# Attention and routed convolution on Trainium2: the split of x formed earlier on ScalarE and GpSimd, the lower filters' products last in each band

## Chip, cores, metric

The kernel runs on one core of one Trainium2 chip (trn2). The metric is the device time of one execution in microseconds, as the median of several runs; smaller is better.

## What is computed

Sixteen images of 128 channels x 32 x 32, f32, go through two residual blocks. Both begin with a group norm (32 groups of 4 channels, without weights). The first is linear attention, the second a convolution whose 3 x 3 filters are mixed from three experts for each image. Cut to what matters:

```
# block 0: x = x + attention(group_norm(x))
xn  = rmsnorm(xg, g1)                          # over the channels
q, k, v = w_qkv @ xn                           # 4 heads of 32
k, v = concat(memory k, k), concat(memory v, v)   # 4 memory tokens
q = softmax(q, over the 32 of a head) * scale
k = softmax(k, over the tokens)
y = rmsnorm(w_out @ (context(k, v) applied to q) + b_out, g2)
# block 1: x = x + condconv(group_norm(x))
y = relu(rconv(pooled 4 x 4) + bias); gates = sigmoid(relu(fc(y)))   # 3 experts x 128
w = sum over experts of gate_k * expert_weight_k                     # per image
x = x + conv3x3(group_norm(x), w)
```

## The kernel before

**Pipeline.** Every engine has its own queue, written out by hand. `run_steps` calls each engine's `step(t, p)` for t = -1 to 20 (steps 9 to 14 as a loop in pairs); a step holds one call per part, `do(part, t, p, age)`, for image t - age, so that an image passes through several steps and each step works on several images. p is the parity of the buffers. Engines meet through semaphores alone. A queue runs strictly in the order in which `step` names its parts.

**The split of x.** Products of f32 numbers are formed on TensorE from an upper and a lower part: `x_hi` is the value rounded to fp32r, `x_lo` the rest. For the normalised input of block 0, ScalarE forms x_hi (`high1`, L591) from xa, and GpSimd forms x_lo (`low1`, L492) as x minus x_hi. high1 waits until the products of qkv of the image before are done, low1 for x_hi and the same. Both are read by the projections (L1160 to L1162).

**ScalarE's queue** around the change: `filters_first` (first expert by its gate, L662), the last two `qkv_evacuate` (qk from PSUM, L601), `results` of the upper band (PSUM plus the group mean, L684; its tile is called expert_raw in the rows, since it reuses that memory), `filters_high` (w_hi, L668), `q_exponent` (L613), `high1` (L591), `squares1`, `k_exponent`, more of `squares1` and `x_copy`, `results` of the lower band.

**GpSimd's queue:** `rms1` (L499), `routing_products` (L527), `x_scale` (L504), rstd and shift, `normalise1` (x, L485), `rms2` (L518), `image_edges` (four zero columns of the shifted images, L544, once the four shifting DMAs of SP have landed), `filters_low` (w_lo = w_full minus w_hi, L537), `low1` (L492), `q_normalise` (L510).

**VectorE's queue,** from the routing on: route_y (L963), the route sums, gates, img_lo, w_second (L1013), k_half (L812), w_full (L1020), q_max (L853), k_quarter (L818), the centre tap plus the identity (L1026), k_max_part (L824), q_exp minus its maximum (L860), k_max, y_scaled (L908), k_exp minus its maximum (L845), q_sum (L868), x of block 0 (L920). w_full, k_quarter, the centre tap, k_max_part and q_exp read two tensors from SBUF each.

**TensorE's queue** begins a step with the transposed second norm (ps_y from y_scaled, L1220), goes on with the convolution (L1282), dealt out in pieces (`conv(n)`) among key contexts, projections, outputs and the routing product (ps_stat, L1227) that route_y waits for. `convolution` yields 9 taps x 3 parts for each of two bands of 16 rows: part 0 is w_hi by the image's upper part, part 1 w_hi by its lower part, part 2 w_lo by its upper part. For images 0 and 15 (`by_pass`) the parts are the outer loop; otherwise the taps are, and the head of the convolution waits for w_lo, img_lo and the edges.

**SP** issues the loads, the shifts (L391 to L395) and the store (L383). load_xa (L368) waits for x_hi of the image whose buffer it takes; it stands behind the previous image's store in the queue.

Of the kernel before, what the change touches and what calls it, by code (L numbers as in the profile page):

```python
# [25 lines left out]
def attention_condconv_kernel(  # L26
# [21 lines left out]
    TAPS = KH * KW  # L48
# [16 lines left out]
    with ctx:  # L65
# [6 lines left out]
        def sem(name):  # L72
            return ctx.enter_context(nc.semaphore(name))
# [212 lines left out]
        w_lo_done = sem("w_lo_done")  # L286
# [20 lines left out]
        def past(b, n):  # L307

            return not isinstance(b, int) or b >= n
# [32 lines left out]
        def turn(part, t, p, age):  # L342

            j = t - age
            if not isinstance(j, int) or 0 <= j < B + GAP:
                part(j, (p - age) % 2)

        def do(part, t, p, age, *args):

            b = t - age  # L350
            if not isinstance(b, int) or 0 <= b < B:
                part(b, (p - age) % 2, *args)

        def once(part, t, at, *args):

            if isinstance(t, int) and t == at:
                part(*args)
# [73 lines left out]
        def _(pool):  # L431
# [115 lines left out]
            def step(t, p):  # L547
                do(rms1, t, p, 3)
                do(routing_products, t, p, 5)
                do(x_scale, t, p, 3)  # L550
                turn(inverse_deviations, t, p, 2)
                do(gn1_shift, t, p, 2)
                do(normalise1, t, p, 2)
                do(rms2, t, p, 4)
                do(image_edges, t, p, 5)
                do(filters_low, t, p, 5)
                do(low1, t, p, 2)
                do(q_normalise, t, p, 3)

            run_steps(pool, step)  # L560

        @block.scalar
        def _(act):
# [128 lines left out]
            def step(t, p):  # L692
                do(gate_exponent, t, p, 4)
                do(qkv_evacuate, t, p, 2, 4)
                do(qkv_evacuate, t, p, 2, 5)
                do(filters_first, t, p, 4)
                do(qkv_evacuate, t, p, 2, 6)
                do(qkv_evacuate, t, p, 2, 7)
                do(results, t, p, 5, 0)
                once(expert_evacuate, t, 2, 0)  # L700
                once(expert_evacuate, t, 2, 1)
                once(expert_evacuate, t, 2, 2)
                once(expert_evacuate, t, 2, 3)
                once(expert_evacuate, t, 3, 6)
                once(expert_evacuate, t, 3, 7)
                do(filters_high, t, p, 4)
                do(q_exponent, t, p, 2)
                do(high1, t, p, 1)
                do(squares1, t, p, 1, 0)
                do(memk_exponent, t, p, 2)  # L710
                do(k_exponent, t, p, 2)
                do(squares1, t, p, 1, 1)
                do(x_copy, t, p, 1, 0)
                do(results, t, p, 5, 1)
                once(expert_evacuate, t, 2, 4)
                once(expert_evacuate, t, 2, 5)
                do(k_x_evacuate, t, p, 2)
                do(x_copy, t, p, 1, 1)
                do(x_k_evacuate, t, p, 2)
                once(expert_evacuate, t, 3, 8)  # L720
                do(q_evacuate, t, p, 2, 0)
                do(qkv_evacuate, t, p, 1, 0)
                do(qkv_evacuate, t, p, 1, 1)
                do(q_evacuate, t, p, 2, 1)
                do(image_high, t, p, 3)
                do(qkv_evacuate, t, p, 1, 2)
                do(qkv_evacuate, t, p, 1, 3)
                do(squares2, t, p, 2)

            run_steps(act, step)  # L730

        @block.vector
# [346 lines left out]
        def _(pe):  # L1079
# [167 lines left out]
            def convolution(b, p):  # L1247

                by_pass = isinstance(b, int) and b in (0, B - 1)
                if by_pass:  # L1250
                    products = [(n, part) for part in range(3) for n in range(TAPS)]
                else:
                    products = [(n, part) for n in range(TAPS) for part in range(3)]
                    pe.wait_ge(w_lo_done, b + 1)
                    pe.wait_ge(img_lo_done, b + 1)
                    pe.wait_ge(edges_done, b + 1)
                bands = ((0, HH), (HH, H))
                if isinstance(b, int) and b == B - 1:
                    bands = LAST_BANDS
                for h, (first_row, end_row) in enumerate(bands):  # L1260
                    bank = (ps_conv[0], ps_conv[1], ps_qkv[0])[h]
                    if h == 2:
                        pe.wait_ge(qkv_done, NT * B)
                    elif past(b, 1):
                        pe.wait_ge(result_done, 2 * (b - 1) + h + 1)
                    for n, part in products:
                        if n == 0 and part == 0 and h == 0:
                            pe.wait_ge(w_hi_done, b + 1)
                            pe.wait_ge(img_hi_done, b + 1)
                        if by_pass and n == 0 and part == 1 and h == 0:  # L1270
                            pe.wait_ge(img_lo_done, b + 1)
                        if by_pass and n == 0 and part == 2 and h == 0:
                            pe.wait_ge(w_lo_done, b + 1)
                        if by_pass and n == KW and part == 0 and h == 0:
                            pe.wait_ge(edges_done, b + 1)
                        tap = TAP_ORDER[n]
                        down = tap // KW - 1
                        top, bottom = max(first_row, -down), min(end_row, H - down)
                        hi, lo = ((left_hi, left_lo), (img_hi, img_lo), (right_hi, right_lo))[tap % KW]
                        into = bank[:, W * (top - first_row):W * (bottom - first_row)]  # L1280
                        weight, pixels = ((w_hi[p], hi[p]), (w_hi[p], lo[p]), (w_lo[p], hi[p]))[part]
                        last = mm(into, weight[:, tap, :], pixels[:, top + down:bottom + down, :],  # L1282
                                  start=(n == 0 and part == 0), stop=(n == TAPS - 1 and part == 2))
                        if n == TAPS - 1 and part == 2:
                            last.then_inc(conv_ps, 1)
                        yield

            def step(t, p):
                convolving = not isinstance(t, int) or OLDEST <= t < OLDEST + B
                products = convolution(t - OLDEST, (p - OLDEST) % 2) if convolving else iter(())  # L1290

                def conv(n):
# [98 lines left out]
```

## Time and profile before

| | before |
|---|---|
| median of 3 runs | 440.47 us (439.46 to 441.87) |
| span of the profiled execution | 438.3 us, 8984 instructions |
| TensorE matmul busy | 414.9 us (95%), 2651 |
| TensorE weight loads | 367.2 us (84%) |
| VectorE busy | 351.1 us (80%), 769 |
| ScalarE busy | 296.2 us (68%), 908 |
| GpSimd busy | 265.0 us (60%), 249 |
| DMA | 61.63 MB, mean 141 GB/s |

The profiled execution has its span as its only time; it lies 2.2 us below the median of the runs, which are timed without the profiler. Busy shares are means over the span: an engine that is 95% busy can still be waiting once in every step, and an engine that is 60% busy can be what a step waits for at one place.

### The profile page before, as it was taken

How to read it: one execution, taken by the hardware profiler on the slowest of the kernel's cores; microseconds unless marked ns; L12 is line 12 of the kernel's file. 1: busy time of each engine (PE TensorE's matmuls, PEld its weight loads, DVE VectorE, ACT ScalarE, POOL GpSimd, SP SyncE). 2: the span in 40 equal slices, each digit the busy share in tenths (PEclk: the TensorE clock that was granted, in tenths of full speed). 3: DMA queues.
4: the chain of work that ended last, by engine and by line, in shares of the span. 5: the costliest groups of instructions: out<-in, count | busy, mean ns of one | idle time of the engine just before them, and what ended most of it. 6: DMA issues, size and time to landing. Idle time of an engine off the chain costs nothing.

```text
span 438.3 us, 8984 instructions
## 1 busy us (share of the span) xinstructions
PE 414.9 (95%) x2651; PEld 367.2 (84%) x2651; DVE 351.1 (80%) x769; ACT 296.2 (68%) x908; POOL 265.0 (60%) x249
## 2 busy tenths in 40 slices
PE   7789898999999999999999999999999999999987
PEld 6688787979898988889797988888898989778777
DVE  3565989797989889797989798898989696987540
ACT  2785857868676858778676868688686868654131
POOL 4754739567583939486674939385874748252330
PEclk9999999999999999999999999999999999999999
DMA  7420242216252442506262433516162523424331
GB/s 195 178 98 2 96 193 98 120 72 241 99 218 119 146 192 95 229 28 228 98 241 96 175 160 126 208 53 230 52 239 96 192 97 114 175 98 191 146 143 48
DMA packets 19075, 61.63 MB, mean 141 GB/s; under 512 B 3024, under 2 KB 4320, under 8 KB 19040
## 3 DMA queue, kind: packets, MB, share of 16 engines
q1 hardware_dynamic: 19040, 61.21, 37.0%
q8 instruction: 16, 0.26, 0.2%
q14 instruction: 19, 0.16, 0.1%
HBM read 19.29 MB, written 8.39 MB: 63 GB/s over the span
## 4 chain that ended last, share of the span: by engine, by line
PE 43%; DVE 22%; issue 17%; ACT 11%; DMA 2%; POOL 1%; DVEq 0%; SPq 0%; ACTq 0%; POOLq 0%
PE ps_conv L1282 13%; PE ps_y L1214 6%; PE ps_att L1181 5%; DVE w_full L1020 5%; ACT expert_raw L662 4%; DVE y_scaled L908 3%; DVE route_terms L974 3%; ACT qk L601 3%; PE ps_y L1204 3%; PE ps_y L1220 3%; DVE q_exp L860 2%; DMA xa<-in_x_dram 2%; ACT squares L574 2%; PE ps_qkv L1160 2%; PE ps_qkv L1162 2%
## 5 line engine op out<-in xcount | busy, mean ns | idle before, releaser
L601 ACT ACTIVATE qk<-ps_qkv,scale 128x256 f32<-128x256 f32 x128 | 55.7, 471 | 5.9 <-PE ps_qkv L1162 3.5
L544 POOL TENSOR_TENSOR left_hi<-zeros 128x32 fp32r<-128x32 f32 x16 | 9.4, 585 | 78.9 <-DMA right_lo<-img_lo 78.9
L668 ACT ACTIVATE w_hi<-w_full 128x1152 fp32r<-128x1152 f32 x16 | 18.7, 1168 | 52.9 <-DVE w_full L1026 52.9
L537 POOL TENSOR_TENSOR w_lo<-w_full,w_hi 128x1152 fp32r<-128x1152 f32 x16 | 42.8, 2675 | 11.0 <-ACT w_hi L668 6.1
L492 POOL TENSOR_TENSOR x_lo<-x,x_hi 128x1024 fp32r<-128x1024 f32 x16 | 38.4, 2399 | 13.1 <-ACT x_hi L591 13.1
L518 POOL TENSOR_TENSOR scale<-ssq,minus_half 128x8 f32<-128x8 f32 x16 | 26.2, 1639 | 32.9 <-DVE ssq L901 32.9
L642 ACT ACTIVATE y_scaled<-ps_y 128x128 f32<-128x128 f32 x128 | 33.5, 294 | 14.5 <-PE ps_y L1214 14.5
L1160 PE MATMUL ps_qkv<-wqk_hi,x_hi 128*128 128x256 f32 x128 | 40.6, 317 | 2.5 <-ACT x_nt L582 1.3
L1282 PE MATMUL ps_conv<-left_lo,w_hi 128*128 128x512 f32 (+2 forms) x96 | 40.6, 424 | 0.0
L1282 PE MATMUL ps_conv<-img_hi,w_hi 128*128 128x512 f32 (+1 forms) x96 | 36.4, 393 | 2.5 <-issue 1.4
L1282 PE MATMUL ps_conv<-right_hi,w_hi 128*128 128x512 f32 (+2 forms) x96 | 37.9, 395 | 0.0
L1282 PE MATMUL ps_conv<-left_hi,w_hi 128*128 128x512 f32 (+2 forms) x96 | 37.1, 388 | 0.0
L1282 PE MATMUL ps_conv<-left_hi,w_lo 128*128 128x512 f32 (+2 forms) x96 | 37.0, 386 | 0.0
L1282 PE MATMUL ps_conv<-right_lo,w_hi 128*128 128x512 f32 (+2 forms) x96 | 37.0, 386 | 0.0
L1282 PE MATMUL ps_conv<-right_hi,w_lo 128*128 128x512 f32 (+2 forms) x96 | 36.9, 385 | 0.0
L1282 PE MATMUL ps_conv<-img_hi,w_lo 128*128 128x512 f32 (+1 forms) x96 | 36.2, 387 | 0.0
L1162 PE MATMUL ps_qkv<-wqk_hi,x_lo 128*128 128x256 f32 x128 | 36.0, 282 | 0.0
L1161 PE MATMUL ps_qkv<-wqk_lo,x_hi 128*128 128x256 f32 x128 | 35.9, 280 | 0.0
L1282 PE MATMUL ps_conv<-img_lo,w_hi 128*128 128x512 f32 (+1 forms) x96 | 35.7, 386 | 0.0
L574 ACT ACTIVATE squares<-ps_qkv 128x128 f32<-128x128 f32 x128 | 32.5, 261 | 0.4 <-PE ps_qkv L1145 0.4
L510 POOL TENSOR_TENSOR q_exp<-q_exp,q_rsum 128x1024 f32<-128x1024 f32 x16 | 30.7, 1921 | 1.9 <-DVE q_rsum L874 1.9
L1214 PE MATMUL ps_y<-mix,q_t 128*128 128x128 f32 x256 | 31.3, 275 | 0.2 <-DVE mix L895 0.2
(172 smaller groups left out, 1337.5 us busy)
## 6 DMA issues: line engine op xcount, KB each, us to landing
xa<-in_x_dram SPq DMA_DIRECT2D x16, 512.0 KB, 4.1
xb<-in_x_dram SPq DMA_DIRECT2D x16, 512.0 KB, 4.7
left_hi<-img_hi SPq DMA_DIRECT2D x16, 511.5 KB, 2.9
right_hi<-img_hi SPq DMA_DIRECT2D x16, 511.5 KB, 3.7
left_lo<-img_lo SPq DMA_DIRECT2D x16, 511.5 KB, 2.9
right_lo<-img_lo SPq DMA_DIRECT2D x16, 511.5 KB, 3.7
out_dram<-expert_raw SPq DMA_DIRECT2D x15, 512.0 KB, 2.9
expert_raw<-_conv_expert_weight_dram SPq DMA_DIRECT2D x1, 1728.0 KB, 9.0
```

Source lines behind the costliest of these rows:

```text
L492: nc.gpsimd.tensor_tensor(x1_lo[:, :], x1[:, :], x1_hi[:, :].bitcast(F32), ALU.subtract).then_inc(x1_lo_done, 1)
L510: nc.gpsimd.tensor_tensor(q_exp[:, :, :], q_exp[:, :, :], q_rsum[:, :].unsqueeze(2).to_broadcast((128, NT * HEADS, DH)), ALU.mult).then_in ...
L518: nc.gpsimd.tensor_tensor(scale2[:, :], ssq2[:, :], minus_half[:, :], ALU.pow).then_inc(scale2_done, 1)
L537: nc.gpsimd.tensor_tensor(w_lo[p][:, :, :].rearrange("p t o -> p (t o)"), w_full[:, :], w_hi[p][:, :, :].bitcast(F32).rearrange("p t o -> ...
L574: last = nc.scalar.activation(squares[:, tile(t)], ps_qkv[h][:, tile(t % (NT // 2))], ACT.Square, accum_out=ssq1_sum[:, t:t + 1])
L601: nc.scalar.activation(qk[:, t, :], ps_qkv[t % 2][:, 0:QK], ACT.Copy, scale=scale1[:, t:t + 1]).then_inc(qkv_done, 1)
L642: last = nc.scalar.activation(y_scaled[:, t, :], ps_y[:, tile(t)], ACT.Square, accum_out=ssq2_sum[:, t:t + 1])
L1160: mm(o, x1_hi[:, tile(t)], wqk_hi[:, :], start=True, stop=False)
L1161: mm(o, x1_hi[:, tile(t)], wqk_lo[:, :], start=False, stop=False)
L1162: mm(o, x1_lo[:, tile(t)], wqk_hi[:, :], start=False, stop=True).then_inc(qkv_ps, 1)
L1214: last = mm(ps_y[:, tile(t)], q_t[p][:, tile(t)], mix[p][:, :], start=True, stop=True)
L1282: last = mm(into, weight[:, tap, :], pixels[:, top + down:bottom + down, :], start=(n == 0 and part == 0), stop=(n == TAPS - 1 and part == 2))
```

## The change

Three edits. On GpSimd `low1` moves from behind `filters_low` to ahead of `image_edges`. On ScalarE `high1` moves from behind `q_exponent` to directly behind the last qkv evacuation, ahead of the first result copy. In TensorE's convolution (all images but 0 and 15) the products of parts 0 and 1 come first, tap by tap, and those of part 2, with w_lo, follow for all taps at the end of each band; the wait for w_lo moves from the head to the first of them. VectorE's and SP's queues stay as they are, and no engine gets more or fewer instructions. TensorE's products of the convolution are on line 1281 of the changed kernel, since the text is a line shorter.

```diff
--- before.py
+++ after.py
@@ -552,9 +552,9 @@
                 do(gn1_shift, t, p, 2)
                 do(normalise1, t, p, 2)
                 do(rms2, t, p, 4)
+                do(low1, t, p, 2)
                 do(image_edges, t, p, 5)
                 do(filters_low, t, p, 5)
-                do(low1, t, p, 2)
                 do(q_normalise, t, p, 3)
 
             run_steps(pool, step)
@@ -696,6 +696,7 @@
                 do(filters_first, t, p, 4)
                 do(qkv_evacuate, t, p, 2, 6)
                 do(qkv_evacuate, t, p, 2, 7)
+                do(high1, t, p, 1)
                 do(results, t, p, 5, 0)
                 once(expert_evacuate, t, 2, 0)
                 once(expert_evacuate, t, 2, 1)
@@ -705,7 +706,6 @@
                 once(expert_evacuate, t, 3, 7)
                 do(filters_high, t, p, 4)
                 do(q_exponent, t, p, 2)
-                do(high1, t, p, 1)
                 do(squares1, t, p, 1, 0)
                 do(memk_exponent, t, p, 2)
                 do(k_exponent, t, p, 2)
@@ -1250,8 +1250,7 @@
                 if by_pass:
                     products = [(n, part) for part in range(3) for n in range(TAPS)]
                 else:
-                    products = [(n, part) for n in range(TAPS) for part in range(3)]
-                    pe.wait_ge(w_lo_done, b + 1)
+                    products = [(n, part) for n in range(TAPS) for part in range(2)] + [(n, 2) for n in range(TAPS)]
                     pe.wait_ge(img_lo_done, b + 1)
                     pe.wait_ge(edges_done, b + 1)
                 bands = ((0, HH), (HH, H))
@@ -1269,7 +1268,7 @@
                             pe.wait_ge(img_hi_done, b + 1)
                         if by_pass and n == 0 and part == 1 and h == 0:
                             pe.wait_ge(img_lo_done, b + 1)
-                        if by_pass and n == 0 and part == 2 and h == 0:
+                        if n == 0 and part == 2 and h == 0:
                             pe.wait_ge(w_lo_done, b + 1)
                         if by_pass and n == KW and part == 0 and h == 0:
                             pe.wait_ge(edges_done, b + 1)
```

ScalarE's queue in the first step that has expert copies and a qk; `experts<-ps_conv` are the expert filters on their way from PSUM:

```order
 L601 ACTIVATE qk<-ps_qkv,scale 128x256 x8
+L591 ACTIVATE x_hi<-xa,shift_1,rstd 128x1024
 L690 ACTIVATE experts<-ps_conv 128x512 x2
 L690 ACTIVATE experts<-ps_conv 128x128
 L690 ACTIVATE experts<-ps_conv 128x512
 L613 ACTIVATE q_exp<-q_exp 128x1024
-L591 ACTIVATE x_hi<-xa,shift_1,rstd 128x1024
```

x_hi passes four expert copies and q_exponent; in steady steps it passes the result copy, w_hi and q_exponent in the same way.

GpSimd's queue in a steady step, from the rms2 power to q_normalise, before:

```order
L518 TENSOR_TENSOR scale<-ssq,minus_half 128x8
L544 TENSOR_TENSOR left_hi<-zeros 128x32
L544 TENSOR_TENSOR left_lo<-zeros 128x32
L544 TENSOR_TENSOR right_hi<-zeros 128x32
L544 TENSOR_TENSOR right_lo<-zeros 128x32
L537 TENSOR_TENSOR w_lo<-w_full,w_hi 128x1152
L492 TENSOR_TENSOR x_lo<-x,x_hi 128x1024
L510 TENSOR_TENSOR q_exp<-q_exp,q_rsum 128x1024
```

and in the changed kernel:

```order
L518 TENSOR_TENSOR scale<-ssq,minus_half 128x8
L492 TENSOR_TENSOR x_lo<-x,x_hi 128x1024
L544 TENSOR_TENSOR left_hi<-zeros 128x32
L544 TENSOR_TENSOR left_lo<-zeros 128x32
L544 TENSOR_TENSOR right_hi<-zeros 128x32
L544 TENSOR_TENSOR right_lo<-zeros 128x32
L537 TENSOR_TENSOR w_lo<-w_full,w_hi 128x1152
L510 TENSOR_TENSOR q_exp<-q_exp,q_rsum 128x1024
```

x_lo has passed the four edge columns, with their wait for the DMAs, and w_lo.

## Rows read from the trace of the kernel before

**Rows 1.** The page, TensorE's granted clock in 40 slices of the span.

```profile
PEclk9999999999999999999999999999999999999999
```

**Rows 2.** Waits view: engine line waited for: us in total, times, longest us.

```profile
DVE route_y L963 <- PE ps_stat L1227: 20.6, 14, 2.7
...
PE ps_y L1220 <- DVE y_scaled L908: 5.5, 15, 0.7
...
PEld ps_conv L1282 <- POOL w_lo L537: 1.9, 3, 1.3
...
PE ps_conv L1282 <- POOL w_lo L537: 1.1, 2, 0.9
```

**Rows 3.** Timeline, VectorE, a steady step: start, length, instruction, [idle before].

```profile
251.83 0.42 DVE L963 TENSOR_TENSOR route_y<-ps_stat,rconv_bias 128x256 f32<-128x256 f32 x1
...
257.90 1.42 DVE L1020 SCALAR_TENSOR_TENSOR w_full<-experts,gate_n,w_second 128x1152 f32<-128x1152 f32 x1
...
260.36 0.44 DVE L818 TENSOR_TENSOR k_quarter<-k_half 128x256 f32<-128x256 f32 x1
...
262.79 1.21 DVE L908 TENSOR_TENSOR y_scaled<-ps_y,scale 128x1024 f32<-128x1024 f32 x1
...
276.05 0.42 DVE L963 TENSOR_TENSOR route_y<-ps_stat,rconv_bias 128x256 f32<-128x256 f32 x1 [0.45 <-PE ps_stat L1227]
```

**Rows 4.** Timeline, TensorE, the same step.

```profile
264.06 1.09 PE L1220 MATMUL ps_y<-ident,y_scaled 128*128 128x128 f32 x8 [0.32 <-DVE y_scaled L908]
```

**Rows 5.** Timeline, ScalarE, the same step.

```profile
255.77 0.89 ACT L601 ACTIVATE qk<-ps_qkv,scale 128x256 f32<-128x256 f32 x2
...
263.42 1.23 ACT L591 ACTIVATE x_hi<-xa,shift,rstd 128x1024 fp32r<-128x1024 f32 x1
```

**Rows 6.** Timeline, SP's DMA issues, the same step.

```profile
269.63 0.35 SPq L368 DMA_DIRECT2D xa<-in_x_dram  x1
```

**Rows 7.** Timeline, GpSimd, the same step.

```profile
260.08 0.26 POOL L544 TENSOR_TENSOR left_hi<-zeros 128x32 fp32r<-128x32 f32 x1 [4.58 <-DMA right_lo<-img_lo]
...
262.46 2.67 POOL L537 TENSOR_TENSOR w_lo<-w_full,w_hi 128x1152 fp32r<-128x1152 f32 x1 [1.31 <-ACT w_hi L668]
265.09 2.42 POOL L492 TENSOR_TENSOR x_lo<-x,x_hi 128x1024 fp32r<-128x1024 f32 x1
```

**Rows 8.** Timeline, GpSimd and VectorE side by side, at two other places.

```profile
28.44 1.91 POOL L510 TENSOR_TENSOR q_exp<-q_exp,q_rsum 128x1024 f32<-128x1024 f32 x1
29.16 1.22 DVE L805 TENSOR_SCALAR ssq<-ssq_sum 128x8 f32<-128x8 f32 x1 [1.35 <-ACT squares L574]
...
65.46 2.07 POOL L544 TENSOR_TENSOR left_hi<-zeros 128x32 fp32r<-128x32 f32 x1 [5.01 <-DMA right_lo<-img_lo]
...
66.21 1.22 DVE L860 TENSOR_TENSOR q_exp<-qk,q_max 128x1024 f32<-128x1024 f32 x1
```

**Rows 9.** Timeline, VectorE beside x_lo of the steady step.

```profile
265.25 1.20 DVE L868 TENSOR_REDUCE q_sum<-q_exp 128x32 f32<-128x1024 f32 x1
```

**Rows 10.** Timeline, the first two steps with a qk: ScalarE, VectorE, GpSimd.

```profile
19.27 0.84 ACT L601 ACTIVATE qk<-ps_qkv,scale 128x256 f32<-128x256 f32 x2 [0.35 <-PE ps_qkv L1162]
...
24.75 1.23 ACT L591 ACTIVATE x_hi<-xa,shift,rstd 128x1024 fp32r<-128x1024 f32 x1
...
21.88 0.42 DVE L818 TENSOR_TENSOR k_quarter<-k_half 128x256 f32<-128x256 f32 x1
...
26.12 2.36 POOL L492 TENSOR_TENSOR x_lo<-x,x_hi 128x1024 fp32r<-128x1024 f32 x1 [6.19 <-ACT x_hi L591]
...
41.90 0.41 DVE L818 TENSOR_TENSOR k_quarter<-k_half 128x256 f32<-128x256 f32 x1
```

**Rows 11.** Timeline, TensorE, into the convolution of image 14.

```profile
406.60 0.38 PE L1282 MATMUL ps_conv<-right_lo,w_hi 128*128 128x480 f32 x1
406.82 0.37 PE L1282 MATMUL ps_conv<-right_hi,w_lo 128*128 128x480 f32 x1
408.11 0.50 PE L1282 MATMUL ps_conv<-img_hi,w_hi 128*128 128x512 f32 x1 [0.92 <-POOL w_lo L537]
```

## The prediction

> **What bounds the kernel now.** I read the page's clock line first, then the waits view, then one steady step in the timeline, engine by engine. TensorE's granted clock is full in all 40 slices [rows 1], its upper level of 2.4 GHz, so no time goes to the clock. The waits view shows where TensorE and VectorE hand over to each other [rows 2]: VectorE's route_y waits for TensorE in 14 steps, and TensorE's ps_y product waits for VectorE's y_scaled in 15. GpSimd has room: in the step below it idles 4.58 us ahead of its first edge column [rows 7].
>
> In the timeline these two handovers close a ring. VectorE runs from route_y at 251.83 to the end of y_scaled, 262.79 + 1.21 = 264.00 [rows 3]; TensorE takes over at 264.06 [rows 4] and frees VectorE's next route_y at 276.05 [rows 3]. So a step is about 12.2 us of VectorE and 12.0 of TensorE, 24.2 in all. In its half VectorE has no gap: what is added to one of its instructions between route_y and y_scaled is added to every step. What is added on ScalarE or GpSimd costs only if it reaches one of these two halves.
>
> **1. x_hi earlier on ScalarE.** Now it starts at 263.42 [rows 5], behind w_hi and q_exponent. In the change it follows the pair of qk evacuations, which ends at 255.77 + 0.89 = 256.66. It takes 1.23, so it runs from about 256.6 to 257.83. The result copy behind it moves by no more than that 1.23. Nothing waits for it soon: its bank is wanted by the next convolution, whose first product comes after ps_y at 264.06. ScalarE is idle after that copy, and w_hi still waits for w_full. Cost nothing, in every steady step; without that idle time it would be up to 1.23.
>
> The load of the next xa waits for x_hi too, but on SP it stands behind the store of the previous image and is issued at 269.63 [rows 6], after today's x_hi, and doesn't come earlier. Ahead of the first store the loads do come earlier, but VectorE's stats wait for none of them there. Nothing.
>
> **2. x_lo earlier on GpSimd.** GpSimd is free after the x of normalise1 and the rms2 power, and waits for the shifted images until 260.08 [rows 7]. x_lo is let go 0.14 us behind x_hi's end, at 257.97 (in the first steps x_hi ends at 24.75 + 1.23 = 25.98 and x_lo, which has waited, starts at 26.12 [rows 10]). It takes 2.42 [rows 7]; alone it would be over at 260.4, in GpSimd's idle time. The edge columns (0.26 each), w_lo (2.67) and q_normalise follow. The edges and w_lo are later than now by at most x_lo's own length; see part 3 for who waits for them.
>
> What the move is charged with is the company it gets. At 257.97 VectorE has just gone over from k_half to w_full (257.90, 1.42) [rows 3], which reads two tensors from SBUF. The trace shows what happens to GpSimd beside such an instruction [rows 8]: the edge column of 65.46 took 2.07 instead of 0.26 and ended at 67.53, 0.1 us after VectorE's q_exp (66.21 + 1.22 = 67.43). And the other way round: VectorE's ssq, eight elements wide, started at 29.16 and took 1.22, to 30.38, that is until GpSimd's q_exp product (28.44 + 1.91 = 30.35) was over. Whoever is second stands still until the first is done. Today's x_lo lies beside q_sum, which is a reduction of 1.20 at 265.25 [rows 9], and both run at their usual length.
>
> The Trainium skill states this as a rule in SBUF — State Buffer, "Who interferes with whom": a VectorE instruction with two inputs in SBUF contends with a GpSimd instruction that reads SBUF, the one issued first keeps the shared ports for the whole instruction, and tensor_reduce never contends. The trace agrees in the rows just named. By this rule the move is a loss; by a reading in which the engines merely share memory it would be free.
>
> So in a steady step: w_full is under way, x_lo waits until it ends at 257.90 + 1.42 = 259.32, reads through q_max (a reduction) and ends at about 259.32 + 2.42 - 0.15 = 261.6 (it has been issued already, so I leave out a start-up of 0.15, my choice). k_quarter, two inputs, wanted to run from 260.36 to 260.80 [rows 3]. It is held until 261.6 and ends at about 261.87: +1.07, with small handovers **+1.1 us**. All of VectorE up to y_scaled moves with it, and so TensorE's ps_y. The bounds are 0 (no hold-up, or x_lo kept out until q_exp is over) and 2.3 (GpSimd first, w_full stands for x_lo's 2.42 less its start). I take 1.1 because w_full starts 0.07 before x_lo's release; worked out in the same way for the other steady steps, the difference lies between -0.01 and 0.09. It counts in the 13 steps in which an x_lo (images 3 to 15) stands beside a w_full: 13 x 1.1 = **+14.3**.
>
> The first images have no w_full there. In the step of the first qk the pair ends at 19.27 + 0.84 = 20.11 [rows 10]; x_hi runs to 21.3, x_lo from 21.4 to 23.8, and k_quarter, due at 21.88 with 0.42, ends at about 24.1 instead of 22.3: 1.8 late. The expert copies and x_transpose are behind x_hi too, and slack at the key contexts hides part; I take +0.85. In the next step k_quarter is due at 41.90 [rows 10] and x_lo by the same sums is in its way from 41.5 to 43.8: +1.8, of which I take 1.75. Together **+2.6** (bounds 0 and 3.6).
>
> **3. Products of w_lo last in each band.** The number of products is the same, and so is their time. Removed is the wait for w_lo at the head: on TensorE it shows twice (1.1 us, longest 0.9) and on its weight load three times (1.9, longest 1.3) [rows 2]. The largest is image 14's: 406.82 to 408.11 is 1.29 where neighbours are 0.22 apart (406.60 to 406.82) [rows 11], and almost all of what is left hangs on it. I take 0.8 of its 1.1, since group means hold TensorE up near there anyway, and 1.9 - 1.3 = 0.6 of the others: **-1.4** (bounds 0 and -1.9). The new wait for w_lo is at the 19th product, 18 x 0.22 = 4 us into the band at least. With x_lo ending at 261.6, the edges kept out by VectorE until its late q_exp is over at 263.5, and then w_lo's 2.67, w_lo is there at 267; its first product comes after 266.7 + 4 = 270.7. Hidden, with 3.7 us to spare. The edges are there at 264.3, and the head of the band wants them at 266.7, also hidden.
>
> **4. k_exponent no longer behind x_hi** in the two steps in which it set TensorE's key contexts: **-0.5** (bounds 0 and one x_hi, 1.2).
>
> **Sum.** +14.3 + 2.6 - 1.4 - 0.5 = +15.0 on the profiled span of 438.3, that is 453.3. The span is 2.2 below the median of the runs, 440.47; with the same distance the forecast is **455.5 us**, 3.4% slower.
>
> **The rivals.**
> *GpSimd first.* x_lo's release and w_full's start are within 0.1 us, so x_lo may read first, in all steps or some. Then w_full stands 2.3 us and k_quarter none: 13 x 2.3 + 2.6 - 1.9 = +30.6, time 471. For it: the margin is small, and right_hi and right_lo of many steps get in between two VectorE instructions. Against: w_full was ahead, or level, in each step.
>
> *No hold-up, or x_lo held until q_exp is over* (not slower). Place: between w_full and k_quarter. If VectorE's chain kept GpSimd out as it did the edge of 65.46 through four instructions [rows 8], or two-input reads did not collide for this pair of shapes, k_quarter would run on time. Left are -1.4 - 0.5 and +0.4 for the expert copies behind x_hi: -1.5, time 439.0, within 0.5% of before. It decides from the point at which x_lo costs a step less than 0.1 us. Against: q_max is a reduction, and q_sum's row shows x_lo reading beside one.
>
> *The clock.* With +1.1 a step TensorE's gap ahead of ps_y grows from 0.32 [rows 4] to about 1.4. If its clock fell to 1.2 GHz for a fifth of the 12 us behind each gap, 2.4 us a step and 13 steps are +31 on top: 487. Against: the gap of 1.29 at 408 left it at full [rows 1, 11].
>
> **Chances.** x_lo behind w_full 0.68, GpSimd first in all steps or part of them 0.17, no loss 0.12, clock 0.03. What a measurement of this kernel can tell from no change is about 0.5%, 2.2 us. Faster by more than that only if the small gains reach their bounds: 0.05. Same: 0.07 of the no-loss case and 0.01 at the low end of the first, 0.08. Slower 0.87. The first case alone spans 449 to 462 (a stall of 0.7 to 1.5 a step); to hold 8 in 10 I go on to 471 for the second, and to 448 below.
>
> **What the new profile would show.** Right: x_lo at about 258 with a mean near 3.6 us instead of 2.40; w_full still 1.42; k_quarter near 1.5 instead of 0.44; TensorE's wait for y_scaled 1.4 a step, and route_y every 25.3 us; no wait for w_lo on TensorE. Wrong: w_full at 3.7 (GpSimd first), k_quarter at 0.44 (no loss), slices of the clock line below 9, or a wait at the 19th product or for the edges that I call hidden.

## The result, and the profile after

The changed kernel takes 460.32 us (median of 4 runs, 458.98 to 465.16), against 440.74 for the kernel before in the same sessions: a ratio of 1.0456, 95% interval 1.0415 to 1.0498. It is slower, as forecast, and inside the range of 448 to 471; the forecast of 455.5 was 4.8 us too low. The profiled execution's span is 459.0 us, 20.7 above that of before.

From the page of the changed kernel, the parts that answer to [rows 1] and to the busy shares of before:

```profile
PE 420.1 (92%) x2651; PEld 371.0 (81%) x2651; DVE 374.5 (82%) x769; ACT 297.2 (65%) x908; POOL 279.3 (61%) x249
...
PEclk8899898999999999999999999999999999999999
```

VectorE has the same 769 instructions and is busy 23.4 us longer; GpSimd's 249 take 14.3 us longer. Nothing was added to either: an instruction that stands still counts as busy. TensorE's clock line has four slices below full, all in the first fifth.

Waits view of the changed kernel, beside [rows 2] (engine line waited for: us in total, times, longest us):

```profile
DVE route_y L963 <- PE ps_stat L1227: 24.3, 16, 2.7
...
PE ps_att L1168 <- DVE k_max_part L824: 18.7, 15, 3.1
...
PE ps_y L1220 <- DVE y_scaled L908: 5.9, 13, 0.7
```

and one line more of the same view of before:

```profile
PE ps_att L1168 <- DVE k_max_part L824: 2.2, 3, 0.9
```

The wait for w_lo is gone from the list. TensorE's new wait isn't where I put it. I expected ps_y to wait 1.4 us a step for y_scaled; that row has hardly moved (5.9 against 5.5). The lost time shows one handover earlier, at the transposed k_max_part, which is the first thing that TensorE needs from VectorE behind k_quarter: 18.7 us in 15 steps, against 2.2 in 3 before.

Where VectorE's time went is in the timeline. Two steps of the changed kernel, VectorE first, to be held against [rows 3]:

```profile
93.90 1.42 DVE L1020 SCALAR_TENSOR_TENSOR w_full<-experts,gate_n,w_second 128x1152 f32<-128x1152 f32 x1
...
96.36 1.49 DVE L818 TENSOR_TENSOR k_quarter<-k_half 128x256 f32<-128x256 f32 x1
...
194.74 3.58 DVE L1020 SCALAR_TENSOR_TENSOR w_full<-experts,gate_n,w_second 128x1152 f32<-128x1152 f32 x1
...
199.37 0.41 DVE L818 TENSOR_TENSOR k_quarter<-k_half 128x256 f32<-128x256 f32 x1
```

and GpSimd's x_lo in the same two steps, against [rows 7]:

```profile
93.94 3.63 POOL L492 TENSOR_TENSOR x_lo<-x,x_hi 128x1024 fp32r<-128x1024 f32 x1 [2.43 <-ACT x_hi L591]
...
194.71 2.40 POOL L492 TENSOR_TENSOR x_lo<-x,x_hi 128x1024 fp32r<-128x1024 f32 x1 [2.44 <-ACT x_hi L591]
```

In the first, w_full starts 0.04 us ahead of x_lo, runs its usual 1.42, and x_lo stands until it is over; x_lo is still reading when k_quarter comes, which takes 1.49 instead of 0.44. In the second, x_lo starts 0.03 us ahead: now w_full stands, 3.58 instead of 1.42, and k_quarter is untouched. The changed kernel has nine steps of the first kind and four of the second. The second is the rival that the prediction calls "GpSimd first".

The span in parts, from the starts of route_y in both traces (13 steps between the first and the fourteenth):

| part | before | after | difference |
|---|---|---|---|
| up to the first route_y | 56.61 | 60.09 | +3.5 |
| nine steps with x_lo second | 218.0 | 227.1 | +9.1, or 1.01 each |
| four steps with x_lo first | 98.2 | 107.1 | +8.9, or 2.2 each |
| from the fourteenth route_y to the end | 65.5 | 64.7 | -0.8 |
| span | 438.3 | 459.0 | +20.7 |

Of the +3.5 up to the first route_y, 0.9 us lie ahead of the first k_quarter, which starts at 22.79 instead of 21.88, behind a stretch in which TensorE's granted clock was lower (0.72 and 0.71 from 6 to 18 us, 1.00 before). The other 2.6 lie behind it: from the start of the first k_quarter to the first route_y are 37.30 us instead of 34.73.

### The profile page after: what moved, and what is told of

The parts are those of the page before. It is cut to its first block, busy times and chain, and to the rows that moved or that the text cites. A ratio compares the mean times of both kernels' runs of the same rounds, so it can differ in the third digit from the quotient of the medians.

```text
span 459.0 us, 8973 instructions
## 1 busy us (share of the span) xinstructions
PE 420.1 (92%) x2651; PEld 371.0 (81%) x2651; DVE 374.5 (82%) x769; ACT 297.2 (65%) x908; POOL 279.3 (61%) x249
## 4 chain that ended last, share of the span: by engine, by line
PE 44%; DVE 30%; issue 17%; ACT 7%; DMA 1%; DVEq 1%; POOL 0%; ACTq 0%
PE ps_conv L1281 14%; PE ps_y L1214 6%; DVE w_full L1020 6%; PE ps_att L1181 5%; DVE k_quarter L818 4%; ACT expert_raw L662 4%; PE ps_y L1220 3%; DVE y_scaled L908 3%; ACT qk L601 3%; DVE route_terms L974 3%; PE ps_y L1204 2%; PE ps_qkv L1160 2%; DVE q_exp L860 2%; PE ps_stat L1227 2%; PE ps_qkv L1162 2%
## 5 line engine op out<-in xcount | busy, mean ns | idle before, releaser
L492 POOL TENSOR_TENSOR x_lo<-x,x_hi 128x1024 fp32r<-128x1024 f32 x16 | 49.1, 3070 | 35.2 <-ACT x_hi L591 35.2
L668 ACT ACTIVATE w_hi<-w_full 128x1152 fp32r<-128x1152 f32 x16 | 18.7, 1167 | 62.5 <-DVE w_full L1026 62.5
L518 POOL TENSOR_TENSOR scale<-ssq,minus_half 128x8 f32<-128x8 f32 x16 | 26.2, 1639 | 32.5 <-DVE ssq L901 32.5
L1281 PE MATMUL ps_conv<-left_hi,w_hi 128*128 128x512 f32 (+2 forms) x96 | 39.4, 412 | 0.0
L1281 PE MATMUL ps_conv<-right_hi,w_lo 128*128 128x512 f32 (+2 forms) x96 | 38.2, 399 | 0.0
L1281 PE MATMUL ps_conv<-left_lo,w_hi 128*128 128x512 f32 (+2 forms) x96 | 37.1, 388 | 0.0
L499 POOL TENSOR_TENSOR scale<-ssq,minus_half 128x8 f32<-128x8 f32 x16 | 26.4, 1653 | 11.9 <-DVE ssq L805 11.8
L1020 DVE SCALAR_TENSOR_TENSOR w_full<-experts,gate_n,w_second 128x1152 f32<-128x1152 f32 x16 | 31.3, 1954 | 0.1
```

The costliest lines, as they stand in the source:

```text
L492: nc.gpsimd.tensor_tensor(x1_lo[:, :], x1[:, :], x1_hi[:, :].bitcast(F32), ALU.subtract).then_inc(x1_lo_done, 1)
L1020: v.scalar_tensor_tensor(w_full[:, :], experts[:, 2, :], gate_n[:, 2:3], w_second[:, :], ALU.mult, ALU.add).then_inc(w_taps_done, 1)
```

## The experiments

**e1: the third edit alone.**

```diff
-                do(low1, t, p, 2)
                 do(image_edges, t, p, 5)
                 do(filters_low, t, p, 5)
+                do(low1, t, p, 2)
...
-                do(high1, t, p, 1)
                 do(results, t, p, 5, 0)
...
                 do(q_exponent, t, p, 2)
+                do(high1, t, p, 1)
```

> Only the third edit: products of w_lo last in each band, both queues of ScalarE and GpSimd as before. If the loss lies between VectorE and GpSimd (my account), this edit alone is a small gain: the waits for w_lo at the head of the convolution vanish, 1.4 us at my estimate, time about 439 (438.5 to 440.5). The rival, that the other order of the products costs TensorE something (in the changed kernel one group of them shows 412 ns instead of 388), makes it slower than before, by up to 96 x 24 ns = 2.3 us.

Measured: 440.75 us against 441.24, ratio 0.9974 [0.9951, 0.9998]. All w_full are at 1.41 or 1.42, and TensorE no longer waits for w_lo. The gain is small: 0.5 us by the medians, 1.1 by the ratio, whose interval goes from 0.1 to 2.2 and has the foreseen 1.4 in it. In the traces, e1 takes 1.2 us less than before from the first route_y to the end (380.5 against 381.7), 0.8 of them behind the fourteenth route_y. The group of products with 412 ns shows here too (411), without a loss. The kernel before has such a group as well, another one (left_lo by w_hi, 424 ns), so it isn't a price of the new order.

**e2: x_lo back behind w_lo, the other two edits kept.**

```diff
                 do(rms2, t, p, 4)
-                do(low1, t, p, 2)
                 do(image_edges, t, p, 5)
                 do(filters_low, t, p, 5)
+                do(low1, t, p, 2)
```

> The changed kernel with x_lo back behind w_lo on GpSimd; x_hi stays early on ScalarE and the products stay reordered. If x_lo beside w_full and k_quarter is the whole loss, it goes: w_full 1.42 and k_quarter 0.44 in every step, route_y every 24.2 us, time 438 to 440. If ScalarE's early x_hi (it pushes the result copy and the expert copies) is a part of the loss, some of it stays: 445 and more for a quarter of it.

Measured: 441.91 us, ratio 1.0011 [0.999, 1.0032], above the 438 to 440 expected. Some 18 us of the changed kernel's 460.32 are gone with this one line, and every w_full is back at 1.41 or 1.42. But k_quarter isn't at its usual length in every step: it takes 2.13 and 2.12 in the first two. GpSimd has no edges and no w_lo there, so x_lo follows x_hi at once wherever it stands in the queue, and k_quarter stands behind it. From e2's timeline, VectorE and GpSimd:

```profile
24.30 2.13 DVE L818 TENSOR_TENSOR k_quarter<-k_half 128x256 f32<-128x256 f32 x1
```

```profile
23.79 2.36 POOL L492 TENSOR_TENSOR x_lo<-x,x_hi 128x1024 fp32r<-128x1024 f32 x1 [2.31 <-ACT x_hi L591]
```

**e3: x_lo's place kept, its read of SBUF taken away.** The kernel leaves out x_lo: zeros stand in its place, so its result lacks the correction by x_lo.

```diff
-                nc.gpsimd.tensor_tensor(x1_lo[:, :], x1[:, :], x1_hi[:, :].bitcast(F32), ALU.subtract)
+                nc.gpsimd.tensor_tensor(spare_column[:, :], minus_half[:, 0:1], minus_half[:, 1:2], ALU.mult)
+                nc.gpsimd.memset(spare_x[:, :], 0.0)
+                nc.gpsimd.memset(x1_lo[:, :].bitcast(F32), 0.0)
```

> The changed kernel, its three edits in place, but x_lo isn't computed: GpSimd writes zeros there (and zeros into 512 further elements), in one instruction each, behind a one-element product that carries the waits; so x_lo's place in the queue and about 1.7 us of GpSimd's time stay, and its long read of SBUF is gone. The correction by x_lo is missing in the result. If the hold-up is in the reads of SBUF, w_full stays at 1.42 and k_quarter at 0.44 in all steps, and the time is 438 to 441. If it is the mere presence of a GpSimd instruction there, or its writes, k_quarter or w_full grow by about the length that is left, and the time stays above 450.

Measured: 437.36 us, ratio 0.9911 [0.9876, 0.9946], and each w_full is 1.41 or 1.42, each k_quarter 0.41 or 0.42. One step of it, GpSimd, then VectorE:

```profile
256.39 1.32 POOL L494 TENSOR_TENSOR spare_column<-minus_half 128x1 f32<-128x1 f32 x1 [2.53 <-ACT x_hi L595]
257.65 0.52 POOL L495 MEMSET spare_x<- 128x512 f32 x1
258.12 0.95 POOL L496 MEMSET x_lo<- 128x1024 f32 x1
```

```profile
256.25 1.41 DVE L1024 SCALAR_TENSOR_TENSOR w_full<-experts,gate_n,w_second 128x1152 f32<-128x1152 f32 x1
...
258.71 0.41 DVE L822 TENSOR_TENSOR k_quarter<-k_half 128x256 f32<-128x256 f32 x1
```

The one-element product reads SBUF and stands behind w_full: 1.32 us for one element, where it takes 0.19 to 0.23 when it starts ahead of w_full (0.19 at 183.56, with w_full at 183.59). The two instructions that only write run at the same time as VectorE's, the second right across the start of k_quarter, and hold nothing. In the four steps in which the product is through first, both lie beside w_full itself, and it keeps 1.41 or 1.42. It is the read that collides. The three edits without the collision are also worth something, 0.9%, though with 0.9 us less work on GpSimd in each step, and without the reads of a real x_lo.

**e4: x_hi, and with it x_lo, 0.2 us later.**

```diff
             def high1(b, p):
+                nc.scalar.activation(spare_column[:, :], zeros[:, 0:1], ACT.Copy)
                 act.wait_ge(shift1_done, b + 1)
```

> The changed kernel with a one-element ScalarE copy ahead of x_hi, so that x_hi and x_lo come about 0.2 us later. In the changed kernel x_lo was ahead of w_full by 0.03 to 0.09 us in four steps (w_full 3.57) and behind it in nine (k_quarter 1.48). If the start decides who stands, x_lo is behind w_full in all 13 steps here: no w_full above 1.5, 13 k_quarters near 1.5, and about 4 x 1.1 = 4 us less than the changed kernel, 455 to 457. If it is chance, or VectorE stands whenever GpSimd asks, the mixture stays, time 460.

Measured: 457.02 us, ratio 1.0355 [1.0311, 1.0399], 3.3 us less than the changed kernel by the medians, where 4 had been expected. 12 of 13 steps have w_full at 1.41; the exception is the first, where both started at 65.88 and w_full took 3.61. Instead of four steps with x_lo first there is one.

**e5: w_full later.**

```diff
+            def pause(b, p):
+                v.tensor_scalar(spare_column[:, :], minus_half[:, 0:1], 1.0, None, ALU.mult)
...
                 do(k_halves, t, p, 1)
+                do(pause, t, p, 3)
                 do(filters_third, t, p, 3)
```

> The changed kernel with a one-element VectorE instruction ahead of w_full, which moves w_full about 0.1 to 0.2 us behind x_lo's release: the opposite of e4. If the start decides, x_lo is first in all 13 steps, w_full takes 3.57 there and k_quarter 0.41: 9 more steps at +1.1 and 13 to 16 times 0.15 for the instruction itself, about 12 us above the changed kernel, 470 to 474. If VectorE keeps winning in most steps whatever the order, about 462.

Measured: 468.39 us, ratio 1.0621 [1.0574, 1.0668]. The expected size, 470 to 474 us, was missed: w_full stood in nine steps, not 13. The added instruction moved w_full by 0.06 us only (it started at 93.99 and w_full at 94.05), and x_lo fell 0.02 to 0.09 us behind w_full in four steps. But the rule that was to be tested came out without an exception. Over the changed kernel and the six experiments in which a whole or half x_lo meets w_full (e4 to e6, e8 to e10), 13 steps each, the start of x_lo minus that of w_full against who stands:

```
                           steps   x_lo start - w_full start, us
w_full at its own length      61   +0.02 to +0.24
w_full held                   30   -0.15 to  0.00
```

**e6: x_hi in its old place in the first two steps with a qk.**

```diff
                 do(qkv_evacuate, t, p, 2, 7)
-                do(high1, t, p, 1)
+                if not isinstance(t, int) or t >= 4:
+                    do(high1, t, p, 1)
...
                 do(q_exponent, t, p, 2)
+                if isinstance(t, int) and t < 4:
+                    do(high1, t, p, 1)
```

> The changed kernel with x_hi in its old place in the first two steps with a qk, before any convolution weights exist; from then on the change is whole. If the first steps cost what the trace shows (first route_y at 60.09 against 56.61: 3.5 us, a part of it at the lower clock), that much comes back, all else stays: 456 to 458. If it is less than 1 us, 460.

Measured: 459.47 us, ratio 1.0424 [1.0389, 1.046], above the 456 to 458 expected. Against the changed kernel that is 0.9 us less by the medians, within the spread of the changed kernel, and 2.4 less by the profiled spans (456.6 and 459.0). The steps themselves tell more. Ahead of the first k_quarter the granted clock differs from one execution to the next: from 18 to 24 us it was 1.00 in before and 0.52 in e7, whose work up to there is the same in the same order, and that k_quarter starts at 21.88 in the one and at 24.48 in the other. From it to the first route_y the traces fall into two groups:

```
                                        us from first k_quarter to first route_y
before, e1, e6, e7: k_quarter free      34.72 to 34.74
changed, e2, e10: two k_quarters held   37.30 to 37.31
```

So the early x_hi and x_lo cost the first steps 2.6 us. Both k_quarters of e6 are at their usual length.

**e7: the best version.** e2 and e6 together: products of w_lo last, x_lo behind w_lo, x_hi early but for the first steps.

```diff
                 do(filters_low, t, p, 5)
+                do(low1, t, p, 2)
...
+                if not isinstance(t, int) or t >= 4:
+                    do(high1, t, p, 1)
```

> x_hi early only from the step of the first convolution weights on (in the first two steps with a qk it stays behind q_exponent), x_lo back behind w_lo, products of w_lo last. e2 showed two k_quarters of 2.12 in the first steps, where x_lo follows x_hi at once, and nothing of the kind later. If those are what e2 lost against e1, both are 0.42 here, and the time is 437.5 to 440, below e2's 441.9. If x_hi's early place itself is what cost e2 its 1.2 us over e1, nothing changes: 441 to 442.

Measured: 438.88 us against 441.72, ratio 0.9934 [0.9911, 0.9957], below both kernels; the interval lies below 1, but the gain is 0.7% only. All k_quarters are between 0.41 and 0.45. So what e2 lost was x_hi's early place in the first steps; in the steady steps the early x_hi cost nothing (13 steps take 315.2 us here, 315.8 in e1, 316.2 before).

**e8: x_lo in two halves.**

```diff
+                nc.gpsimd.tensor_tensor(x1_lo[:, 0:512], x1[:, 0:512], x1_hi[:, 0:512].bitcast(F32), ALU.subtract)
+                nc.gpsimd.tensor_tensor(x1_lo[:, 512:N], x1[:, 512:N], x1_hi[:, 512:N].bitcast(F32), ALU.subtract)
```

> The changed kernel with x_lo in two instructions of 512 elements each. If an engine keeps the shared path for one instruction at a time, whichever VectorE instruction is second stands for one half only, about 1.1 us: w_full at most 2.5 instead of 3.57, k_quarter of the first steps at most 1.6 instead of 2.13 unless the second half also gets in ahead of it. In the steps where w_full is first, the first half fits beside q_max and k_quarter meets the second: 0.4 or 1.5. Time 448 to 458. If the engines are held until GpSimd's queue is empty, w_full stays at 3.57 and k_quarter at 2.13, time 460.

Measured: 454.48 us, ratio 1.0296 [1.0254, 1.0337]. Where GpSimd is first, w_full now takes 2.45 to 2.48, and the k_quarters of the first steps 1.04 and 1.05 (with k_max_part, which meets the second half, at 1.25 behind the first of them). From its timeline, VectorE and GpSimd:

```profile
192.08 2.48 DVE L1021 SCALAR_TENSOR_TENSOR w_full<-experts,gate_n,w_second 128x1152 f32<-128x1152 f32 x1
```

```profile
192.05 1.29 POOL L492 TENSOR_TENSOR x_lo<-x,x_hi 128x512 fp32r<-128x512 f32 x1 [2.44 <-ACT x_hi L592]
193.30 2.40 POOL L493 TENSOR_TENSOR x_lo<-x,x_hi 128x512 fp32r<-128x512 f32 x1
```

w_full stands for the first half and gets in between the two, and the second half stands in its turn. So the hold-up lasts for one instruction of the other engine, not until its queue is empty. In the other nine steps the price stays, one instruction further on: k_quarter gets through at 0.42 and the centre tap takes 1.36.

**e9: k_quarter from one tensor.**

```diff
-                v.tensor_tensor(k_quarter[:, :, :], k_half[:, 0:NT // 4, :], k_half[:, NT // 4:NT // 2, :], ALU.max)
+                v.tensor_reduce(k_quarter[:, :, :], k_half[:, :, :].rearrange("p (a b) c -> p b c a", a=2), AX.X, ALU.max)
```

> The changed kernel with k_quarter formed as a reduction of one tensor (the maximum of two elements each) instead of an operation on two. If only instructions that read two SBUF tensors are held, k_quarter isn't held any more, in the first steps too, and takes one length of 0.4 to 0.8 everywhere; x_lo's end then holds the next one with two inputs, the centre tap or k_max_part, for what is left, some 0.5 us in the steady steps and 1.3 in the first. If any VectorE instruction is held, k_quarter shows 1.5 to 1.8 in 9 steps and 2.1 and more in the first.

Measured: 459.43 us, ratio 1.0417 [1.0374, 1.046]. k_quarter is 0.68 or 0.69 in all 16 steps, and the next instruction that reads two tensors takes the blow. From its timeline, VectorE, a steady step and the first one with a qk:

```profile
94.67 0.69 DVE L818 TENSOR_REDUCE k_quarter<-k_half 128x256 f32<-128x512 f32 x1
95.27 0.75 DVE L1026 TENSOR_TENSOR w_full<-w_full,ident 128x128 f32<-128x128 f32 x1
...
21.98 0.69 DVE L818 TENSOR_REDUCE k_quarter<-k_half 128x256 f32<-128x512 f32 x1
22.70 1.28 DVE L824 TENSOR_TENSOR k_max_part<-k_quarter 128x128 f32<-128x128 f32 x1
```

x_lo was reading through the whole of both k_quarters (from 92.25 to 95.88, and from 21.47 to 23.83). A reduction of one tensor isn't held by it. That isn't shown for every instruction with one tensor: the ssq of [rows 8], a TENSOR_SCALAR of one tensor of eight elements, took 1.22 beside a GpSimd product, and four more of the 16 in the trace of before took 0.45 to 0.80 instead of 0.15 to 0.19.

**e10: the first two edits with the old order of the products.** The wait for w_lo and the products are those of the kernel before.

> Edits 1 and 2 alone; the products stay in the old order, with the wait for w_lo at the head of the convolution. In the changed kernel w_lo ends at 102.23 in the second full step, and the head product starts at 102.00; so the old order would wait about 0.2 us a step in nine steps, and about 0.8 at image 14, which gives 462 to 464. If the reorder hid nothing, 460.

Measured: 462.54 us, ratio 1.0514 [1.0466, 1.0563]. The time is in the expected interval, but the reason isn't the expected one: no steady step's product waits for w_lo. The waits view has image 14's only:

```profile
PE ps_conv L1282 <- POOL w_lo L537: 0.9, 1, 0.9
```

Within the changed kernel the third edit is thus worth the 0.9 us at image 14. The medians are 2.2 us apart, with ranges that overlap and executions at different granted clocks; the one execution of each at a mean clock of 0.996 had spans of 458.4 and 457.3, which are 1.1 apart.

**e11: x_lo early, x_hi late.**

```diff
-                do(high1, t, p, 1)
                 do(results, t, p, 5, 0)
...
                 do(q_exponent, t, p, 2)
+                do(high1, t, p, 1)
```

> Edits 1 and 3 alone: x_lo ahead of the edges on GpSimd, but x_hi in its old place, so GpSimd waits for x_hi until about 264.65 of the step of before, with the edges, w_lo and q_normalise behind it. x_lo then lies beside q_sum again, so w_full is 1.42 and k_quarter 0.44 in all steps. The edges are there at 268.1 instead of 261.2, the convolution's head wants them at 265.6: at least 2.5 us a step from the queue alone, 12 to 13 steps, time 470 to 478. If the loss of the changed kernel came from GpSimd's order and not from where x_lo runs, this one would be near 460.

Measured: 482.4 us, ratio 1.0926 [1.0859, 1.0993], beyond my upper end. No w_full or k_quarter is held. GpSimd waits for x_hi 133.7 us in 16 steps, and the edges are now late for the convolution:

```profile
PE ps_conv L1281 <- POOL right_lo L544: 17.1, 7, 2.6
```

A step takes 27.6 us (12 steps from the route_y at 85.19 to that at 415.88) instead of 24.2. Six of the 40 clock slices are below full here, so a part of it is clock. This is a loss of another kind: a queue's order, not a collision. The changed kernel avoids it by moving x_hi too, so its own loss isn't this one.

## Why the forecast held, and where it was off

**The ring.** Right. VectorE's half of the step grew and the step with it. Each hold-up between w_full and y_scaled reached the time: steps of the first kind grew by 1.01 us and those of the second by 2.2. Only the handover at which TensorE waits was another: k_max_part, not y_scaled.

**x_hi earlier: nothing.** Right for the steady steps: with x_lo back in place and the first steps left alone (e7) the early x_hi is in a kernel that is faster than before.

**x_lo beside VectorE.** The mechanism was right and is shown: taking away the read takes away the loss (e3), a reduction of one tensor isn't held (e9), the hold-up is per instruction (e8), and who starts first runs (e4, e5 and the table). The Trainium skill's SBUF — State Buffer, "Who interferes with whom", says the same in each point: two inputs in SBUF against a GpSimd instruction that reads, not one that only writes; the whole instruction; the order of issue decides. One of the two examples that the prediction read from [rows 8] isn't a case of the two-input rule, though: ssq reads one tensor (see e9). It shows that GpSimd can hold VectorE, not that this takes two inputs.

**The step that failed** is the one that made a single case of it: "w_full is under way, x_lo waits", 13 times 1.1. The prediction saw that the two starts lay within 0.1 us of each other, took from the steps of before that w_full was ahead or level, and priced all 13 steps by that. In the changed kernel the difference ran from -0.09 to +0.13, with four steps on the other side. They cost 8.9 us instead of 4 x 1.1 = 4.4: +4.5.

Most of this could be read from the steps of before. The prediction let x_hi start 0.06 us ahead of the end of the last pair of evacuations; in the changed kernel it starts 0.10 to 0.11 ahead. With this value its own sum, worked out again, puts x_lo ahead of w_full in five of the 13 steps of before, by some 0.05 us and, in the first, 0.08. (In that first step x_lo is ahead by 0.04 even with 0.06, so "in each step" was misread.) The four steps of the changed kernel with x_lo first are four of these five; in the fifth it came 0.05 behind.

The rest of the distance is small and partly cancels: +0.9 from the clock ahead of the first k_quarter, +0.5 from the first steps, +0.6 from the products, and -0.8 from nine steps that were a little cheaper. With the +4.5 that is the 5.7 us between the span of 453.3 that was worked out and the 459.0 of the trace. The prices of a hold-up were good: 1.07 to 1.1 foreseen and 1.01 measured, 2.3 foreseen and 2.2 measured. The range held because its upper end had been put there for the rival of 13 steps with x_lo first; a mixture of the two orders had been named as possible but not priced.

**The first steps.** Both k_quarters stood as foreseen (2.13 instead of 0.42, so +1.7 each against 1.8). From the first k_quarter to the first route_y that made 2.57 us. The sum had 2.6 for them and took 0.5 off for k_exponent, which the early x_hi lets go sooner in the same two steps. TensorE's idle time ahead of the key contexts did shrink there, from 1.14 and 1.27 us to 0.40 and 0.55, but 2.57 is what was left with that gain in it. So the two terms together were 0.5 too low; no run takes them apart.

**Products last.** The wait for w_lo vanished, as said. By itself the term was about right: e1's trace gains 1.2 us behind the first route_y, against 1.4. In the changed kernel only the 0.8 at the end is left of it, since the steady steps wouldn't have waited for w_lo there even in the old order (e10).

**The clock,** which I gave 0.03: it did fall, only not in the steady steps. In the windows of the changed kernel around its first meeting of x_lo and w_full (us, then TensorE, weight load, VectorE, ScalarE, GpSimd busy, granted clock, DMA share, GB/s):

```profile
68.00:74.00 6.00, 2.46 (x18) 2.06 (x17) 5.96 (x9) 1.97 (x2) 2.52 (x6) 0.96 0.48 179
74.00:80.00 6.00, 6.00 (x37) 5.56 (x36) 5.93 (x9) 4.03 (x20) 3.73 (x2) 0.76 0.00 1
```

TensorE had waited 3.12 us for k_max_part, up to 72.08, and then got 1.2 GHz for some 3 us (0.73, 0.50, 0.50 and 0.56 in the four windows of 1 us from 73 on). In the other three steps of that kind it waited too, 1.84 us in the one at 200.24, and the clock stayed at 2.4 GHz. The profile of before has no such slice, but e1 and e7 have slices below full in their first 24 us as well, so a part of this belongs to the first steps of any version; why it comes in some executions and not in others stays open. The spread of the changed kernel's four executions goes with it too: with a mean clock of 0.996, 0.993, 0.985 and 0.971 their spans are 457.3, 458.1, 459.0 and 463.4. By that, of the 20.7 us between the two profiles one or two are clock, as an estimate.

## What to carry to other kernels

Before moving a GpSimd instruction into idle time, look at what VectorE does there: beside an instruction that reads two SBUF tensors it isn't idle time, and GpSimd's idle time costs nothing while VectorE's standstill may cost every step. Good company is a reduction (q_max, and k_quarter in e9), or an operation with one input in PSUM: before, y_scaled and w_lo overlap from 262.79 to 264.00 [rows 3, 7], and both have their usual length. One tensor alone is no promise, as ssq shows. Where two engines' instructions start within 0.1 us of each other, price both orders step by step: a few hundredths of a microsecond in the working decide who comes first, and the steps can fall on both sides.

## What I had not expected of the hardware

The order of two starts decided who stood, down to 0.01 us (the traces' last digit), with no exception in 91 steps; in the three steps with a difference of 0.00 w_full stood. And the smallest reader pays as much as a large one: one element on GpSimd took 1.32 us beside w_full, against 0.19 alone.
